# Weight splits of a fused decoder layer: seventeen pairs ahead of the expert loop instead of thirteen, and the router spread over its units

## The reference

```python
x = x + attn(layernorm(x))        # 16 heads of 8; convolved queries and keys; scores * tau + delta
x = x + xattn(layernorm(x), ctx)  # 16 heads of 8, keys masked per sequence
x = x + ffn(layernorm(x))

# ffn: router over E = 64 experts in 8 groups, the best 4 groups by the sum of their two best scores, then the best 8 experts
coef = zeros(T, E).at[rows, topk_idx].add(topk_w)      # 8 of 64 are not zero
g, u = einsum('th,ehi->tei', x, Wg), einsum('th,ehi->tei', x, Wu)
h = silu(g) * u * coef[:, :, None]
out = einsum('tei,eih->th', h, Wd) + silu(x @ SWg) * (x @ SWu) @ SWd
```

## Time and profile before

| | us |
|---|---|
| median of 3 runs | 321.78 (316.3 to 324.49) |
| profiled execution | 317.97 |
| its span | 316.2 |
| TensorE busy | 289.7 (92%) |
| VectorE busy | 236.4 (75%) |
| ScalarE busy | 194.5 (62%) |
| GpSimd busy | 172.9 (55%) |
| attention steps | about 38 to 157 |
| expert units, first half | about 157 to 241 |
| expert units, second half | about 241 to 310 |

### The profile page before, as it was taken

The page is one execution under the profiler, slowest core; times in us unless marked ns, Lnnn a source line. Parts: engine busy times, 40 slices in busy tenths (PEclk is TensorE's granted clock), DMA queues, the critical chain, the costliest instruction groups (busy, mean ns, idle before and its releaser), DMA issues.

```text
span 316.2 us, 5282 instructions
## 1 busy us (share of the span) xinstructions
PE 289.7 (92%) x1672; PEld 203.7 (64%) x1672; DVE 236.4 (75%) x502; ACT 194.5 (62%) x353; POOL 172.9 (55%) x222
## 2 busy tenths in 40 slices
PE   1999996999999999699979999599999999999995
PEld 1634764666555555455655766478778888888883
DVE  3895894789859887788894659999866666666663
ACT  2796944786884666367553797367555455555553
POOL 8230070020710299829139589699996566666662
PEclk9999977999999999999999999799999999999999
DMA  7820677176251214540101526466633433444421
GB/s 271 239 35 1 217 134 150 35 260 141 45 125 33 46 23 129 139 111 8 44 0 42 188 84 209 138 177 204 204 120 114 119 120 136 128 133 133 129 70 67
DMA packets 29627, 37.16 MB, mean 118 GB/s; under 512 B 5024, under 2 KB 17952, under 8 KB 29600
## 3 DMA queue, kind: packets, MB, share of 16 engines
q1 hardware_dynamic: 29600, 36.84, 41.2%
HBM read 28.43 MB, written 3.93 MB: 102 GB/s over the span
## 4 chain that ended last, share of the span: by engine, by line
PE 49%; POOL 16%; DVE 12%; ACT 7%; DMA 6%; issue 5%; SPq 3%; POOLq 0%; DVEq 0%; ACTq 0%
PE bank L455 34%; POOL qbd L1530 6%; POOL stacks L1501 6%; PE bank L828 3%; PE bank L829 3%; PE bank L830 3%; DMA stacks<-stacks 3%; SPq L407 2%; POOL xn L295 2%; DMA pa<-pack_a 2%; DVE conv L1419 2%; PE bank L575 2%; DVE vs L1427 1%; PE bank L600 1%; DMA coefficient_rows<-ctxs 1%
## 5 line engine op out<-in xcount | busy, mean ns | idle before, releaser
L455 PE MATMUL bank<-khl,stacks 128*128 128x512 f32 x396 | 102.9, 396 | 6.4 <-DVE conv L1419 4.6
L1530 POOL TENSOR_TENSOR qbd<-vs,qbd 128x512 fp32r<-128x512 f32 x65 | 84.3, 1299 | 36.2 <-ACT qbd L1056 36.1
L455 PEld LDWEIGHTS bank<-khl,stacks 128*128 128x128 f32 x396 | 73.7, 190 | 25.3 <-issue 9.9
L1419 DVE TENSOR_TENSOR conv<-bank,conv 128x512 f32<-128x512 f32 x61 | 42.1, 690 | 31.9 <-ACT bank L1030 31.5
L1030 ACT ACTIVATE bank<-bank 128x512 f32<-128x512 f32 x62 | 36.1, 582 | 40.8 <-PE bank L455 40.7
L1175 DVE TENSOR_REDUCE rawmax<-bank 128x4 f32<-128x512 f32 x64 | 43.2, 684 | 13.9 <-PE bank L455 12.9
L1056 ACT ACTIVATE qbd<-vs 128x512 fp32r<-128x512 f32 x66 | 41.2, 624 | 18.2 <-DVE vs L1427 12.5
L455 PE MATMUL bank<-stacks 128*128 128x512 f32 x96 | 41.9, 486 | 3.3 <-DMA stacks<-stacks 2.8
L1427 DVE TENSOR_TENSOR vs<-conv,bank 128x512 f32<-128x512 f32 x62 | 42.6, 687 | 2.1
L958 ACT ACTIVATE conv<-bank 128x512 f32<-128x512 f32 x64 | 34.9, 595 | 6.5 <-PE bank L455 5.5
L1501 POOL TENSOR_TENSOR stacks<-ring,stacks 128x384 fp32r<-128x384 f32 x33 | 34.4, 1043 | 1.0
(11 more groups left out here) (186 smaller groups left out, 432.9 us busy)
## 6 DMA issues: line engine op xcount, KB each, us to landing
conv<-coefficient_rows SPq DMA_DIRECT2D x122, 128.0 KB, 2.9
ring<-w SPq DMA_DIRECT2D x33, 192.0 KB, 2.7
stacks<-stacks SPq DMA_DIRECT2D x68, 64.0 KB, 2.1
stacks<-split_rows SPq DMA_DIRECT2D x16, 192.0 KB
split_rows<-stacks SPq DMA_DIRECT2D x6, 256.0 KB, 2.6
split_rows<-khl SPq DMA_DIRECT2D x3, 512.0 KB, 3.6
pa<-pack_a SPq DMA_DIRECT2D x1, 706.0 KB, 5.3
xres<-x SPq DMA_DIRECT2D x1, 512.0 KB, 4.0
```

Source lines behind the costliest of these rows:

```text
L455: return pe.matmul(out, lhsT, rhs, start=start, stop=stop)
L1419: dve.tensor_tensor(out, gate, spread[:, n % ROWS, :, :], ALU.mult).then_inc(gate_scaled, 1)
L1530: pool.tensor_tensor(hlo[:, n % 4, :].rearrange("p (b t) -> p b t", b=4), hx[n % 4], hhi[:, n % 4, :].bitcast(F32).rearrange("p (b t) -> p ...
```

## The change

- `EARLY_PAIRS` goes from 13 to 17. The order of the arrays in `stacks` changes, so that pairs 0 to 4 lie in spare memory and in the split keys, which are free once these have been stacked. GpSimd now splits pairs 0 to 4 before the first of the two norms of cross-attention, 5 to 10 between them, 11 to 16 after the second.
- The ring loads of the attention part stand at steps 5 to 15, one to three a step (`PAIR_LOADS`).
- In the expert loop the remaining 16 pairs are split in two units of every three: 4, 5, 7, 8, 10, 11 to 26 (`split_unit`; the low part in GpSimd's next unit), and the pair five further on is loaded at SyncE's turn three later (`load_unit`).
- The second router's functions are cut into single operations, one or two behind each unit from 8 to 27. The computation is the same.

```diff
-EARLY_PAIRS = 13
-AHEAD = 8
+EARLY_PAIRS = 17
+PAIR_LOADS = {5: (5,), 6: (6,), 7: (7, 8), 8: (9,), 11: (10,), 12: (11, 12), 13: (13, 14, 15), 14: (16, 17),
+              15: (18, 19, 20)}
...
-        stack_sizes = (("kst0", G * T), ("khl0", 2 * T), ("qhl", 2 * T), ("pick", 4 * G * P), ("kst1", G * T), ("qst", G * T),
-                       ("kbd", 2 * G * J * P), ("spare", 22 * P))
+        stack_sizes = (("spare", 22 * P), ("khl0", 2 * T), ("kst0", G * T), ("qhl", 2 * T), ("pick", 4 * G * P), ("kst1", G * T),
+                       ("qst", G * T), ("kbd", 2 * G * J * P))
...
+        split_unit = {FIRST + i + i // 2: EARLY_PAIRS + i for i in range(PER_HALF - EARLY_PAIRS)}
+        load_unit = {n + 3: pair + RING for n, pair in split_unit.items() if pair + RING < PER_HALF}
...
-                if s == 12:
-                    for pair in range(RING, 2 * RING):
-                        load(pair)
-                if s == 14:
-                    for pair in range(2 * RING, EARLY_PAIRS):
-                        load(pair)
+                for pair in PAIR_LOADS.get(s, ()):
+                    load(pair)
...
-            for pair in range(EARLY_PAIRS, EARLY_PAIRS + RING):
-                load(pair)
+            load(EARLY_PAIRS + RING - 1)
             rows_out(0)
             for n in range(FIRST, UNITS):
...
                 if n != PER_HALF:
                     coefficient_rows(n)
-                if EARLY_PAIRS + RING <= n + AHEAD < PER_HALF:
-                    load(n + AHEAD)
+                if n in load_unit:
+                    load(load_unit[n])
...
-                if EARLY_PAIRS <= n + AHEAD < PER_HALF:
-                    high_weights(n + AHEAD)
+                if n in split_unit:
+                    high_weights(split_unit[n])
...
-            SECOND_ROUTER = {8: score_with_bias, 10: first_round, 12: last_rounds, 14: compare_groups, 16: rank_groups,
-                             18: mask_groups, 20: pick_eight, 22: keep_scores, 24: sum_scores, 26: coefficients}
             for n in range(FIRST, UNITS):
                 unit(n)
-                if n in SECOND_ROUTER:
-                    SECOND_ROUTER[n](1)
+                if n == 8:
+                    score_with_bias(1)
+                if n == 9:
+                    first_maxima(1)
...
+                if n == 15:
+                    least_high(1, 1)
+                    greatest_low(1, 1)
...
+                if n == 23:
+                    find_eight(1)
+                if n == 24:
+                    take_eight(1)
+                if n == 25:
+                    keep_scores(1)
+                if n == 26:
+                    sum_scores(1)
+                if n == 27:
+                    coefficients(1)
...
-            pool.wait_ge(ld_b, 16)
-            for c in range(2):
+            def normalise_again(c):
+
                 normalise(pool, link, 1, 4 * c, 4 * c + 4, False)
                 add_bias(pool, Bw("bo"), 4 * c, 4 * c + 4, B + 4 * c + 4)
...
+            pool.wait_ge(k_stacked, G)
+            pool.wait_ge(rows_put[0], 48)
+            for pair in range(RING):
+                early_weights(pair)
+            pool.wait_ge(ld_b, 16)
+            normalise_again(0)
             pool.wait_ge(exped, G * B)
             pool.wait_ge(maxima_got, 128)
-            pool.wait_ge(rows_put[0], 48)
-            for pair in range(8):
+            for pair in range(RING, 2 * RING + 1):
                 early_weights(pair)
+            normalise_again(1)
             pool.wait_ge(q_stacked, 3 * G)
             pool.wait_ge(rows_put[1], 48)
-            for pair in range(8, EARLY_PAIRS - 2):
+            for pair in range(2 * RING + 1, EARLY_PAIRS):
                 early_weights(pair)
             normalise(pool, link, 2, 0, 4, False)
-            for pair in range(EARLY_PAIRS - 2, EARLY_PAIRS):
-                early_weights(pair)
             low_inputs(0)
...
-                if EARLY_PAIRS <= n + AHEAD - 1 < PER_HALF:
-                    pool.wait_ge(whi_ready, n + AHEAD - EARLY_PAIRS)
-                    low_weights(n + AHEAD - 1)
+                if n - 1 in split_unit:
+                    pair = split_unit[n - 1]
+                    pool.wait_ge(whi_ready, pair + 1 - EARLY_PAIRS)
+                    low_weights(pair)
```

More of the change, by code:

```diff
@@ L1216, in _, with router_space, scratch @@
             NG = HB * GE
-            taken = [HE]
-            def scratch(n):
-                taken[0] += n
-                return flat_k[:, taken[0] - n:taken[0]]
-            pairs = lambda w: scratch(NG * w).rearrange("p (n e) -> p n e", e=w)
-            a4, b4 = pairs(4), pairs(4)
-            rounds = [(w, [pairs(w) for _ in range(4)]) for w in (2, 1)]
-            gs, rank, wsum = scratch(NG).rearrange("p (b g) -> p b g", g=GE), scratch(NG), scratch(HB)
+            def router_space(*spaces):
+                spaces = [list(space) for space in spaces]
+                def scratch(n):
+                    space = next(space for space in spaces if space[1] + n <= space[2])
+                    space[1] += n
+                    return space[0][:, space[1] - n:space[1]]
+                pairs = lambda w: scratch(NG * w).rearrange("p (n e) -> p n e", e=w)
+                biased = scratch(HE)
+                a4, b4 = pairs(4), pairs(4)
+                rounds = [(w, [pairs(w) for _ in range(4)]) for w in (2, 1)]
+                gs, rank, wsum = scratch(NG).rearrange("p (b g) -> p b g", g=GE), scratch(NG), scratch(HB)
+                return biased, a4, b4, rounds, gs, rank, wsum
+            in_sbuf = (flat_k, 0, B * (P + 2))
+            router = [router_space(in_sbuf)] * 2
+            equal, lower = [gcmp[:, 1, :, :, :]] * 2, [gcmp[:, 2, :, :, :]] * 2
             half_of = lambda c: slice(HB * c, HB * c + HB)
@@ L1271, in compare_groups, with find_equal @@
                 own = gs.unsqueeze(3).broadcast_to([P, HB, GE, GE])
-                note(dve.tensor_tensor(gcmp[:, 0, :, :, :], other, own, ALU.is_gt))
-                link(dve.tensor_tensor(gcmp[:, 1, :, :, :], other, own, ALU.is_equal))
-            def rank_groups(c):
+                note(dve.tensor_tensor(above, other, own, ALU.is_gt))
+            def find_equal(c):
+                gs = router[c][4]
+                other = gs.unsqueeze(2).broadcast_to([P, HB, GE, GE])
+                own = gs.unsqueeze(3).broadcast_to([P, HB, GE, GE])
+                link(dve.tensor_tensor(equal[c], other, own, ALU.is_equal))
@@ L1276, in rank_groups, with find_lower, add_lower @@
+            def find_lower(c):
                 dve.wait_ge(ones_ready, 2 + GE)
                 lowb = low[:, :, :].rearrange("p g f -> p (g f)").unsqueeze(1).broadcast_to([P, HB, GE * GE])
-                link(dve.tensor_tensor(f2(2), f2(1), lowb, ALU.mult))
-                link(dve.tensor_tensor(f2(0), f2(0), f2(2), ALU.add))
+                link(dve.tensor_tensor(flat_f(lower[c]), flat_f(equal[c]), lowb, ALU.mult))
+            def add_lower(c):
+                link(dve.tensor_tensor(flat_f(above), flat_f(above), flat_f(lower[c]), ALU.add))
@@ L1302, in sum_scores @@
             def sum_scores(c):
+                wsum = router[c][6]
                 link(dve.tensor_reduce(wsum, coef[:, :, :], AX.X, ALU.add))
```

105 lines of the change are left out of this document (79 added, 26 removed).

## The result

| | before | changed |
|---|---|---|
| median of 6 runs each | 320.4 (316.3 to 324.49) | 321.42 (320.58 to 326.07) |
| profiled execution | 317.97 | 324.76 |
| its span | 316.2 | 322.1 |
| products of unit 0 to products of unit 29 | 76.2 | 82.4 |

The ratio of the times is 1.0101, 95% interval 1.0052 to 1.0149: about 3.2 us slower, within 2%. The medians are of all six executions and lie 1.0 apart; the ratio compares only executions that were not in a slower state of the chip, so it is not their quotient. Forecast were 325.0 and no change that can be told.

A forecast was written before the change was run, and what follows sets the result against it. TensorE was taken to set the pace in the second expert half, VectorE's and GpSimd's delays slowing the first. Experts +5.3 and attention -0.6 made +4.7 us on 319.9: 324.6, rounded 325, range 315 to 332.

The forecast's parts named there:

- Ring-load loop: Expert loop: low weights, ring load, coefficient rows, gate scaling close in 8.3 us per three units against 6.12; unit 23 5.7 later.
- Tail behind unit 23: Expert units 23 to 29: router operations take 11.2 us, products of unit 29 start 5.85 later, taken as 5.3.
- Blocked ring loads: Attention step 12 to 13: SyncE no longer blocks on five loads, so the next product starts 1.6 us sooner.
- Early splits: Attention: weight splits on GpSimd slow VectorE's cast of the maxima in two more steps, 0.5 each, 1.0 us slower.
- rival C: Attention: early splits cost more than their blocked loads gave, through port waits in every such step; +3, 328 us, chance 0.10.
- Attention together: -1.6 + 1.0 = -0.6: Whole attention part: 1.6 us gained from unblocked loads, 1.0 lost to early splits; range -1.6 to +0.8.
- A: Expert loop: coefficient rows never late, TensorE at 2.04 a unit, -6.9 there; 312.4 us on the forecast's footing, chance 0.16.
- the 3.70 wait: First expert half before the change: TensorE's largest idle time, 3.70 us, released by unit 13's gate scaling, expected to go.
- B: Expert loop: the forecast with TensorE's clock falling in the loop's idle times; +8, 333 us, chance 0.12.
- the 2.77 wait: Attention step 13 before the change: TensorE idles 2.77 us for key blocks behind five ring loads; expected to go.

The follow-up runs named there:

- The doubled work: The changed kernel with GpSimd's low part of pairs 5 to 9 made twice, in its idle time: 321.56 us, ratio 1.0115 to the kernel before.

## Why the prediction was right, and where it was not

**Ring-load loop: right, to some tenths.** (Its pace of 2.04 was read from units 31 and 32, the last of the first half; in the second half the kernel before has it too, 250.67 to 252.71.) Forecast were turns of 8.3 from 186.1 to 227.6; the trace has 8.40 to 8.51, and one of 9.56, from 184.64 to 228.01. The start came 1.5 early because GpSimd's unit 5 began at 178.39 and not at 179.91 as before. That is not the change's doing: unit 0 started 0.3 earlier, and the write of the first half's rows, behind which the first coefficient rows wait, took 2.3 instead of 3.75 in this execution, so that unit 4 was scaled at 173.71 and not at 175.34. The long turn is one slow transfer: the rows issued by 198.40 were there at 202.6, 4.1 after, the maximum of the earlier trace rows, where the sum had the median. The two misses cancel, by luck. Both the removal of the loop (-9.4 on the stage) and its insertion into the kernel before (+6.6) confirm it as the cause. An estimate from those starts: with a write of 2.3 the stage before would have been some 1.3 to 1.4 shorter, so the loop costs nearer 7.5 than 6.2.

**Tail behind unit 23: right.** 239.15 was worked out for the products of unit 29, and they started at 239.20, from a unit 23 that came 0.4 late and a tail of 11.2 for the 11.55 of the working. The sum took 5.3 out of 5.85, on the ground that GpSimd is less busy there; that discount was not borne out. The stage as a whole is 6.2 longer.

**Blocked ring loads: right in size.** The steps of the splits from 12 to 13 went from 8.0 to 6.8, 1.2 of the 1.6 forecast in this pair of profiles. In the two other profiled kernels with the old loads it was 9.5 and 9.2, so the gain is rather 1.2 to 2.7. The difference goes with the clock: TensorE waited 2.76 to 2.77 in all three, and in those two the granted clock then fell (0.81, 0.50, 0.83 in the stretches from 130 to 136 us with the earlier loads, 0.87, 0.50, 0.77 from 128 to 134 with the spread router), while before the change it stayed 1.00.

**Early splits: about right in sum, but not as told.** Steps 8 to 11 take 19.6 instead of 18.6, the 1.0 forecast. The doubled work shows that it doesn't grow with GpSimd's load; the prediction's price per split step, and rival C with it, had the wrong variable. The changed kernel's own trace has 0.9 more than this sum: the split of the maxima at 85.12 comes 6.5 after the one before it instead of 5.2, and the next gives back 0.3. In the ten kernels made from it that step takes 5.2 to 5.9, and why it was longer here stays open.

**Two terms were missing in the attention part.** The step that failed is "Attention together: -1.6 + 1.0 = -0.6". It left out pair 10's late load, +1.2 between two splits of the maxima, and the shift of the row gathers, -4.3 by the run that undoes it alone. How much it is in all can be read from the starts of the products of unit 0 in the profiled executions: 159.3 on average in the three kernels with all of the old attention (157.14 to 160.86), 155.6 in the six with the new one (153.60 to 157.84), 154.4 in the four that also have pair 10 early (152.38 to 156.60). So the attention gained about 3.7, not 0.6, and +6.2 - 3.7 = +2.5 stands beside the measured +3.2. The pair of profiles that the prediction had would have hidden this: its own kernel before, at 157.14, was the earliest of three. The forecast of +4.7 was near because the loop outweighed everything, and the discount on the tail covered a part of what the attention was short of.

**Rivals.** A had the 3.70 wait right, not the rest: even with the rows in time, at four and five turns, the stage is 3.2 to 3.9 shorter than before (72.95 and 72.3 for 76.16), not 6.9, since other waits of 0.3 to 1.5 stay; what the whole gained beyond that came from the attention part. B did not happen as a state. Windows of the changed kernel with busy times and, ahead of the last two columns, the granted clock:

```profile
202.00:204.00 2.00, 0.56 (x1) 0.50 (x2) 1.36 (x3) 0.00 (x0) 0.00 (x0) 0.73 0.47 170
204.00:206.00 2.00, 2.00 (x6) 1.61 (x5) 1.56 (x5) 1.21 (x3) 1.24 (x2) 0.50 0.35 97
206.00:208.00 2.00, 2.00 (x9) 1.62 (x9) 1.97 (x4) 1.24 (x3) 2.00 (x3) 0.92 0.00 0
208.00:222.00 14.00, 11.51 (x48) 8.27 (x48) 10.57 (x15) 7.15 (x14) 8.83 (x9) 1.00 0.51 164
```

After the 2.74 idle the clock stood at the 1.2 GHz level for some 3.4 us, as the three stretches add up, the six products took 2.90, and the slack of the turn absorbed it; the waits of 0.8 to 1.6 in the later turns left it at 1.00. The prediction had applied the Trainium skill, "TensorE: Matmul & The Clock Gate", section "HAM oscillation — how this bites in real kernels", outside what it describes: the kernel there waits some 3 to 5 us for transfers at every tile, longer than any wait of this loop, so the section does not make B the rule here.

This verdict holds for the expert loop only. In the attention part the clock did fall, and for longer, before the change as after it; the prediction looked at it nowhere there but at the 2.77 wait. The changed kernel's own windows behind its wait of 0.90 at 53.83:

```profile
54.00:56.00 2.00, 2.00 (x14) 1.78 (x14) 1.57 (x3) 1.16 (x2) 0.00 (x0) 1.00 0.95 133
56.00:58.00 2.00, 2.00 (x27) 0.97 (x29) 1.45 (x6) 0.61 (x2) 0.00 (x0) 0.54 0.81 156
58.00:60.00 2.00, 2.00 (x20) 1.29 (x13) 0.55 (x1) 1.10 (x4) 0.00 (x0) 0.61 0.65 108
```

The scatter of the attention part goes with this: with the new order of the gathers the clock fell there in 3 of 10 profiled kernels (the changed one, and those with loads at n + 5 and with pair 10 early), and those three have the longest steps in this place (8.7, 10.7 and 8.4 between splits; at most 7.3 in the others).

**What stays open.** Why the clock falls behind a wait of some length in one execution and not in the next. The waits behind the gathers were 0.90, 1.28 and 1.16 in the three where it fell, and 0.98, 1.07, 1.02 and 1.15 in four where it did not; at step 12 it fell after 2.76 in two kernels and not after 2.77 in a third.

## What to carry to other kernels

When a load is moved closer to the event that frees its buffer, close the loop before anything else: from the freeing event through every queue that the load blocks (here the coefficient rows behind it) back to the next such event, and compare it with the pace of the bound engine for as many units. One more unit of distance was worth 3% here and cost one number. A list of single steps in an in-order transfer queue deserves the same count for every entry, the small ones too: a gather moved by one step, which the prediction did not count, was worth some 4 us, and a prefetch put one step late held the norm behind it.

## What the runs showed of the hardware that was not expected

- VectorE's cast of 128x16 takes 0.17 alone and up to 0.94 beside GpSimd's work in the changed kernel, but 5 us more of that work in the same stretch gave three casts of 0.49, 0.80 and 0.42 instead of one of 0.94 and one of 0.36, with the same sum of steps.
- In the expert loop TensorE's granted clock fell after every wait of 1.96 us or more, nine in eight profiled kernels (six products in 2.90 after 2.74), each time for some 3.4 us, and after none of 1.92 or less. In the attention part length does not sort them: the clock fell behind waits of 2.0 to 2.8 in all four cases at the first gather and after 0.90 to 1.28 in three of seven, for 3.4 to 10 us; in step 12 after 2.76 in two kernels and not after 2.77. A step with such a fall grew by more than its wait: 4.9 with a wait of 2.79, 4.6 with one of 1.28 (10.7 for 6.1).
- A transfer of coefficient rows took 4.1 instead of 2.9 once in the profiled execution, and in an in-order loop this one delay was passed on: the turns behind it kept their 8.4 to 8.5. The write of the first half's rows, 128 KB, landed after 2.3 in most executions and after 3.6 to 4.1 in four, which moved the start of the loop by 1.3 to 1.6.
